# Turning 42 of 128 attention-probability blocks by DMA in a perceiver block, with GpSimd splitting and merging the 16-bit halves

## The reference, cut to what matters

```python
q, k, v = split_heads(LN(x) @ Wq + bq), split_heads(ctx @ Wk + bk), split_heads(ctx @ Wv + bv)
attn = softmax(einsum('bhqd,bhkd->bhqk', q, k) / sqrt(32))     # 2 x 16 x 128 x 2048
x = x + merge_heads(einsum('bhqk,bhkd->bhqd', attn, v)) @ Wo + bo
x = x + LN(self_attention(LN(x)) + LN(x)) * gamma + beta       # 16 heads, T = 128
x = x + LN(ffn_one_of_4_experts(x) + x) * gamma + beta         # 512 -> 2048 -> 512
```

## Time and profile before

| | |
|---|---|
| median of 3 runs (lowest to highest) | 510.3 us (509.75 to 511.0) |
| the profiled execution | 509.62 us, of which span 507.8 us |
| busy: PE, PE weight loads, DVE, ACT, POOL | 492.1, 380.6, 303.8, 265.0, 42.2 us |
| mean granted TensorE clock | 0.997 of full speed |

### The profile page before, as it was taken

One profiled execution on the slowest core, in us unless ns is written; L12 is line 12 of the kernel. 1 busy time (PEld: TensorE's weight loads), 2 busy tenths in 40 slices (PEclk: granted clock), 3 DMA queues, 4 the chain that ended last, 5 costly groups with the idle time before them and its releaser, 6 DMA issues.

```text
span 507.8 us, 9274 instructions
## 1 busy us (share of the span) xinstructions
PE 492.1 (97%) x3754; PEld 380.6 (75%) x3754; DVE 303.8 (60%) x585; ACT 265.0 (52%) x402; POOL 42.2 (8%) x34
## 2 busy tenths in 40 slices
PE   8999998999999999999999999989999999999995
PEld 6786777777777777898887777756686767888673
DVE  4637542645565452256168475668379988998932
ACT  4131027485767732327447757567337565677510
POOL 0220000000099000000000000000002010000000
PEclk9999999999999999999999999999999999999998
DMA  8900000000242002220120000099367799795000
GB/s 286 357 0 1 1 1 0 2 1 1 88 166 82 1 23 108 101 103 0 52 95 2 2 1 1 1 388 421 121 258 286 305 382 409 256 374 201 1 14 28
DMA packets 11353, 62.47 MB, mean 123 GB/s; under 512 B 1584, under 2 KB 2096, under 8 KB 4528
## 3 DMA queue, kind: packets, MB, share of 16 engines
q1 hardware_dynamic: 11024, 61.62, 31.7%
q10 hardware_dynamic: 288, 0.27, 0.2%
HBM read 61.36 MB, written 0.52 MB: 122 GB/s over the span
## 4 chain that ended last, share of the span: by engine, by line
PE 86%; ACT 7%; issue 3%; DVE 2%; POOL 0%; POOLq 0%; ACTq 0%; DVEq 0%
PE ps L1153 36%; PE ps L1223 11%; PE ps L1237 6%; PE ps L1207 6%; ACT Pm L453 4%; PE ps L1474 3%; PE ps L1476 3%; PE ps L1475 3%; PE ps L1418 3%; PE ps L1428 2%; PE ps L1430 2%; PE ps L1429 2%; PE ps L1147 1%; PE ps L1493 1%; ACT PT L461 1%
## 5 line engine op out<-in xcount | busy, mean ns | idle before, releaser
L752 DVE TENSOR_SCALAR_CACHE_REDUCE Pm<-ps,small 128x512 f32<-128x512 f32 x96 | 66.4, 749 | 30.4 <-PE ps L1207 30.3
L461 ACT COPY PT<-ps 128x512 f32<-128x512 f32 x128 | 68.5, 592 | 29.0 <-PE ps L1223 29.0
L1223 PE MATMUL ps<-ident,Pm 128*128 128x128 f32 x512 | 69.3, 277 | 3.2 <-ACT Pm L453 3.2
L1223 PEld LDWEIGHTS ps<-ident,Pm 128*128 128x128 f32 x512 | 56.5, 141 | 18.0 <-issue 11.0
L453 ACT ACTIVATE Pm<-Pm,small 128x2048 f32<-128x2048 f32 x32 | 64.3, 2010 | 3.5 <-DVE Pm L752 3.5
L732 DVE SCALAR_TENSOR_TENSOR KrL<-ps,small,KrH 128x512 fp32r<-128x512 f32 x32 | 23.9, 748 | 61.3 <-ACT KrH L439 61.3
L1153 PE MATMUL ps<-wvH,ctxH 128*128 128x512 f32 x124 | 50.6, 408 | 1.0 <-DVE V L741 1.0
L1153 PE MATMUL ps<-ctxH,wkH 128*128 128x512 f32 x124 | 51.1, 412 | 0.0
L1153 PE MATMUL ps<-ctxL,wkH 128*128 128x512 f32 x124 | 48.6, 392 | 0.0
L1153 PE MATMUL ps<-ctxH,wkL 128*128 128x512 f32 x124 | 48.5, 391 | 0.0
L1153 PE MATMUL ps<-wvH,ctxL 128*128 128x512 f32 x124 | 48.4, 390 | 0.0
(11 more groups left out here) (231 smaller groups left out, 876.6 us busy)
## 6 DMA issues: line engine op xcount, KB each, us to landing
w1raw<-in_W SPq DMA_DIRECT2D x16, 1024.0 KB, 6.1
w2raw<-in_W SPq DMA_DIRECT2D x15, 1024.0 KB, 5.0
raw<-in_ctxT SPq DMA_DIRECT2D x7, 1024.0 KB, 7.1
woF<-in_ffn_Wo SPq DMA_DIRECT2D x4, 1024.0 KB, 9.0
wo<-in_wo SPq DMA_DIRECT2D x2, 1024.0 KB, 4.7
ctx_first<-in_ctxT SPq DMA_DIRECT2D x4, 256.0 KB, 4.8
wv_raw<-in_xWv SPq DMA_DIRECT2D x2, 512.0 KB, 7.2
wq<-in_xWq SPq DMA_DIRECT2D x1, 1024.0 KB, 12.2
```

Source lines behind the costliest of these rows:

```text
L461: act.copy(PT[:, c % 2, i, :, :].rearrange("p k t -> p (k t)"), ps[:, t_bank(p, c, i), :]).then_inc(pt_done, 1)
L752: dve.tensor_scalar(Pm[:, i, c * CH:(c + 1) * CH], ps[:, i, :], -1.0, mx[:, p % 2, i, c - 1:c] if c else NOT_YET, ALU.mult, ALU.min, accum ...
L1223: last = pe.transpose(ps[:, t_bank(p, c, i), j * P:(j + 1) * P], Pm[:, i, c * CH + j * P:c * CH + (j + 1) * P], ident[:])
```

## The change

1. **Turns by DMA.** For passes 0 to 6, chunks 2 and 3 (`PEC` = 2), heads 0 to 2 (`HD` = 3), the turn is no longer made by TensorE. GpSimd takes the 512 floats of a head and chunk apart into 512 low and 512 high 16-bit halves (`probs_split`, into `stage`, one buffer for each of the two chunks), SyncE issues a DMA with transposition of the 128x1024 halves back into the same place of `Pm` (`turned`), and GpSimd puts the halves together again in `PT` (`probs_merged`). The next scores of that chunk now wait for the merge. Head 3 and chunks 0 and 1, and pass 7, stay as they were.
2. **Keys.** In rounds 1, 2, 3, 5, 6 and 7 VectorE makes the high part of chunks 0 and 1 too. The ring `KrH`, `KrL` has two slots in place of three.
3. **Second context.** ScalarE issues its loads and makes its high parts, VectorE the low parts, in halves, in gaps of rounds 3 and 4.
4. **Orders.** TensorE's weighted values of chunks 2 and 3 come at the start of the next round; 8 of the 12 matmuls of keys 0 of rounds 2, 3, 6 and 7 come before the last scores of the round before. VectorE makes keys 2 and 3 after the drains of chunks 0 and 1. Copies of `outputs2_T(0, ...)` move from VectorE to ScalarE. A few semaphores are merged.

```diff
-        KR = 3
+        KR = 2
+        stage = at("stage", [P, 2, 2, CH], U16, 184)
+        def by_dma(p, c, i):
+            return p < NP - 1 and c >= PEC and i < HD
+        def turned_before(p, c, i):
+            if p == NP - 1 or c < PEC:
+                return PE_TURNS * p + HPG * c + i
+            return PE_TURNS * p + HPG * PEC + (HPG - HD) * (c - PEC) + i - HD
+        def slot_user(p, c):
+            return C * p + c - 1
+        def halves_of(ap):
+            return ap.bitcast(U16).rearrange("p (n h) -> p n h", h=2)
 # SyncE
-            for c in range(C):
-                sp.wait_ge(k_mm, C * (G - 1) + c + 1)
-                sp.dma_start(raw[c][:], a["ctxT"][C + c]).then_inc(raw_in[c], 16)
+            def turned(p, i):
+                for c in range(PEC, C):
+                    sp.wait_ge(p_split, 2 * (HD * p + i) + c - PEC + 1)
+                    sp.dma_start_transpose(Pm[:, i, c * CH:(c + 1) * CH].bitcast(U16).rearrange("p (k t) -> p k t", t=T),
+                                           stage[:, c - PEC, :, :].rearrange("p h n -> p (h n)")).then_inc(p_turned[c], 16)
+            for p in range(G):
+                for i in range(HD):
+                    turned(p, i)
 ...
+            turned(G, 0)
             for k, w in enumerate(("wk", "wv")):
                 sp.wait_ge(qkv_mm[0], k + 1)
                 sp.dma_start(wS[:], a[w]).then_inc(wS_in, 16)
+                turned(G, k + 1)
 ...
+            for p in range(G + 1, NP - 1):
+                for i in range(HD):
+                    turned(p, i)
             sp.wait_ge(k_mm, NP * C)
             first_in_(0)
 # GpSimd
-            for c in range(C):
-                pool.wait_ge(raw_in[c], 32 if c else 16)
-                pool.tensor_copy(ctxH[c][:], raw[c][:]).then_inc(ctx_hi1, 1)
-                pool.wait_ge(ctx_hi1, c + 1)
-                pool.tensor_tensor(ctxL[c][:], raw[c][:], ctxH[c][:].bitcast(F32), ALU.subtract).then_inc(ctx_split1, 1)
+            def probs_split(p, i):
+                pool.wait_ge(exp_done, HPG * p + i + 1)
+                for c in range(PEC, C):
+                    if HD * p + i:
+                        pool.wait_ge(p_turned[c], 16 * (HD * p + i))
+                    words = halves_of(Pm[:, i, c * CH:(c + 1) * CH])
+                    pool.tensor_copy(stage[:, c - PEC, :, :], words.rearrange("p n h -> p h n")).then_inc(p_split, 1)
+            def probs_merged(p, c, i):
+                pool.wait_ge(p_turned[c], 16 * (HD * p + i + 1))
+                if i == 0:
+                    pool.wait_ge(pv_mm, slot_user(p, c))
+                words = halves_of(PT[:, c % 2, i, :, :].rearrange("p k t -> p (k t)"))
+                halves = Pm[:, i, c * CH:(c + 1) * CH].bitcast(U16).rearrange("p (h n) -> p h n", h=2)
+                pool.tensor_copy(words.rearrange("p n h -> p h n"), halves).then_inc(merged[c], 1)
+            for p in range(NP - 1):
+                probs_split(p, 0)
+                probs_split(p, 1)
+                if p == G + 1:
+                    rsqrt(LN3[0])
+                probs_split(p, 2)
+                for i in range(HD):
+                    probs_merged(p, PEC, i)
+                if p == G + 1:
+                    rsqrt(LN4[0])
+                for i in range(HD):
+                    probs_merged(p, PEC + 1, i)
+                if p == G - 1:
+                    rsqrt(LN2[0])
 # ScalarE: keys 0 and 1 only in round G; outputs2_T(0) takes all four heads
+            def context_in(c):
+                act.wait_ge(k_mm, C * (G - 1) + c + 1)
+                act.dma_start(raw[c][:], a["ctxT"][C + c]).then_inc(raw_in[c], 16)
+            def context_high(c, parts=(0, 1)):
+                act.wait_ge(raw_in[c], 32 if c else 16)
+                for h in parts:
+                    k = slice(HALF * h, HALF * (h + 1))
+                    act.copy(ctxH[c][:, k, :], raw[c][:, k, :]).then_inc(ctx_hi1, 1)
                 exponentials(p - 1, 0)
+                if p == G:
+                    context_high(3)
+                if p == G:
                     keys(p, 0)
+                if p == G - 1:
+                    context_in(0)
 ...
+                if p == G - 1:
+                    context_in(2)
+                    context_high(0, (0,))
 ...
+                            if p == G - 1:
+                                context_in(3)
 ...
+                    if p == G - 1 and c == 1:
+                        context_high(0, (1,))
+                    if p == G - 1 and c < 3:
+                        context_high(c)
 # VectorE
+                if p and p != G and c < 2:
+                    dve.wait_ge(k_mm, n + 1)
+                    dve.wait_ge(s_mm, (n - KR + 1) * HPG)
+                    dve.tensor_scalar(KrH[:, c % KR, :], ps[:, bank, :], bias3[:, 1, p % G:p % G + 1], None,
+                                      ALU.add).then_inc(k_hi, 1)
 ...
+                    if p and by_dma(p - 1, c, i):
+                        dve.wait_ge(merged[c], HD * (p - 1) + i + 1)
+                    elif p:
+                        dve.wait_ge(t_mm, turned_before(p - 1, c, i) + 1)
 ...
+            def context_low(c, parts=(0, 1)):
+                for h in parts:
+                    k = slice(HALF * h, HALF * (h + 1))
+                    dve.wait_ge(ctx_hi1, 2 * c + h + 1)
+                    dve.tensor_tensor(ctxL[c][:, k, :], raw[c][:, k, :], ctxH[c][:, k, :].bitcast(F32),
+                                      ALU.subtract).then_inc(ctx_split1, 1)
 ...
+                        if c < 2:
+                            keys(p, c + 2)
 # TensorE, a round with keys
+            EARLY = 8
 ...
+                    keys(p, 0, (EARLY if early_keys(p) else 0, 3 * KT))
                 if late:
+                    weighted_values(p - 2, C - 2)
                     weighted_values(p - 2, C - 1)
                     reciprocals_T(p - 2)
 ...
+                    probs_T(p - 1, 0, 0)
+                    probs_T(p - 1, 0, 1)
+                    keys(p, 2)
+                    probs_T(p - 1, 0, 2)
+                    probs_T(p - 1, 0, 3)
+                    scores(p, 0)
+                    probs_T(p - 1, 1, 0)
+                    probs_T(p - 1, 1, 1)
+                    weighted_values(p - 1, 0)
+                    probs_T(p - 1, 1, 2)
+                    probs_T(p - 1, 1, 3)
+                    scores(p, 1)
+                    weighted_values(p - 1, 1)
+                    keys(p, 3)
+                    probs_T(p - 1, 2, 3)
+                    if p == G + 3:
                         masks(0)
+                    scores(p, 2)
+                    probs_T(p - 1, 3, 3)
+                    if early_keys(p + 1):
+                        keys(p + 1, 0, (0, EARLY))
+                    scores(p, 3)
                 if p == G:
+                    while_values(0)
+                    weighted_values(p - 1, C - 2)
                     weighted_values(p - 1, C - 1)
-                    while_values(0)
```

More of the change, by code:

```diff
@@ L239, in perceiver_block @@
         s_mm, s_done = sem("s_mm"), sem("s_done")
+        p_split = sem("p_split")
+        merged = {c: sem(f"merged{c}") for c in range(PEC, C)}
+        p_turned = {c: sem(f"p_turned{c}") for c in range(PEC, C)}
         exp_done, t_mm = sem("exp_done"), sem("t_mm")
@@ L530, in values2, with outputs2_T @@
                 act.copy(V2[b][:].rearrange("p g d -> p (g d)"), ps[:, 4 * b, :]).then_inc(v2_ready, 1)
-            def outputs2_T(b):
+            def outputs2_T(b, heads):
                 act.wait_ge(cN_ready, b + 1)
-                for i in range(2, HPG):
+                for i in heads:
                     for a in range(HPG):
@@ L992, in alongside @@
                     outputs2(0)
[L993 to L996 removed]
+                if p == G + 1 and at_point == 3:
                     residual2(0)
@@ L1037, in _ @@
                     outputs(p - 2)
+                if p == G:
+                    context_low(3)
                 alongside(p, "keys1")
-                if p < NP:
-                    keys(p, 2)
                 for c in range(C):
@@ L1043, in _ @@
                         negative_scores(p, c)
-                        if c == 1:
-                            keys(p, 3)
+                        if p == G - 1 and c == 1:
+                            context_low(0, (1,))
+                        if c < 2:
+                            keys(p, c + 2)
+                        if p == G - 1 and c == 0:
+                            context_low(0, (0,))
+                        if p == G - 1 and c == 3:
+                            context_low(1)
                     if c == 2:
@@ L1154, in product, with keys @@
                 return mm
-            def keys(p, c):
+            def keys(p, c, part=(0, 3 * KT)):
                 b, g = divmod(p, G)
                 if b:
-                    pe.wait_ge(ctx_split1, c + 1)
+                    pe.wait_ge(ctx_split1, 2 * (c + 1))
                 else:
@@ L1169, in keys @@
```

(53 more changed lines are left out.)

93 lines of the change are left out of this document (46 added, 47 removed).

## The result

The changed kernel takes 503.52 us (four runs, 501.86 to 504.21), the one before, run beside it on the same chip, 510.48 (509.75 to 511.0). The ratio is 0.9864, with a 95% interval of 0.9848 to 0.9881: faster by 1.4%, 7.0 us. The forecast was 494.5, so the sign is right and the size is less than half of it. The profiled execution took 503.49 us with a span of 501.7; before these were 509.62 and 507.8. The sum of the prediction was -15.8 us against that execution, the measured difference is -6.1, and 9.7 us are to be explained.

A forecast was written before the change was run, and what follows sets the result against it. TensorE's own work was taken to bound each round. Against 509.6 us, -21.4 - 2.2 + 1.2 + 2.6 + 3.0 + 1.0 = -15.8 gave 493.8, or 494.5 for the median; range 488 to 514.

The forecast's parts named there:

- The turns' price: TensorE, seven passes: 42 turns leave at 0.51 us each, -21.4 us in all, 3.1 us a round.
- The stall before head 3: Rounds 1 to 3: TensorE's wait for exponentials before the turn of head 3 goes, -2.2 us.
- y: GpSimd's time for one split or merge copy of 1024 halves, taken as 1.0 us, upper bound 2.3.
- L: Landing time of one transposing DMA, taken as 4 us; beyond 5.2 each us costs 3 us a round in six rounds.
- rivals 2 and 3: Rounds: 2, round trip late, L 5.2 to 6.4, 506 us, chance 0.20; 3, slower, landing time, 520 us, chance 0.20.
- a sign of being wrong: Chunks 2 and 3: drains wait for GpSimd's merges, seen as TensorE idle before scores 3.
- The 56 ns of a piece: Transposing DMA: time per 256-byte piece from ScalarE's queue, giving 3.6 us for 1024 pieces, 5.6 with landing.
- 0.2 us a round: End of each round: last head of scores 3 waits for VectorE's drains until 23.9; +1.2 us in the sum.
- Weighted values and early keys are only moved.: TensorE's order: moving these pieces leaves its work unchanged, so no time was added or taken for it.
- the loads (1.5 for contention) and ScalarE's work (1.5): Round 3: context loads share DMA engines, +1.5; ScalarE's load issues +0.8 and high parts +0.7; +3.0 together, 0 to 6.
- The term of +2.6: Round 4: exponential 3 ends at 13.4, not 10.3, behind ScalarE's context part and keys; TensorE waits 3.0 instead of 0.4.
- the load term (0 to 2): Round 7: experts' loads start 5 to 6 us before the first product, not 10.1, and land in 6.1; +1.0 us.

The follow-up runs named there:

- filler run: Changed kernel plus eight needless one-block transposes on TensorE before the last scores of rounds 4 and 7: 501.23 us, ratio 0.9821 to the kernel before.

## Why the prediction was right and wrong

**Right: what bounds a steady round.** "A round is then 24.5 us of TensorE's work": round 2 is 24.57, TensorE busy for 24.52, and the forecast for it was 24.7. The turns' price holds in every round, -21.5 against -21.4. The stall before head 3 went.

**Right: the round trip is hidden in a steady round.** y was taken as 1.0 and is 1.04 at least, 1.16 on average for a split and 1.39 for a merge. L was taken as 4 and is 3.2. Both are far from the point where the cover is gone (L = 5.2), so rivals 2 and 3 did not come to be in the steady rounds. Round 3 is the exception: with landings of up to 6.3 us its drains of chunk 2 stood still for merges (they start 1.2 us apart in place of 0.67, and TensorE waits three times 0.7 us before the last scores), a sign of being wrong that the prediction named. The 56 ns of a piece were too high: the changed page's queues (packets, bytes in MB, share of sixteen engines) are
```profile
q1 hardware_dynamic: 54800, 68.44, 42.7%
q10 hardware_dynamic: 864, 4.46, 2.5%
```
and before they had 31.7% and 0.2%. So 45.2% of 501.7 less 31.9% of 507.8 is 64.8 us of sixteen engines for 42 x 1024 = 43,008 pieces, about 24 ns each (an estimate, for the shares are of whole kernels). The page's rule, beside which the prediction set 10.5 us for a DMA (the Trainium skill, "VectorE: DVE Perf Modes", The three transpose paths), is not borne out by this trace if blocks are taken one after another: eight land in 3.2 us, so they overlap.

**Wrong, 1: no term for the clock (6.6 us).** This is the largest step that failed. The forecast counted TensorE's work at 2.4 GHz throughout, since every window before had 1.00. It also accepted that TensorE would wait before the last scores ("the last head of scores 3 waits for that. That is tight"), and priced such a wait at 0.2 us a round. The waits themselves were 0.7 us in rounds 4 and 7 and 2.2 in round 3; what the half speed adds is 1.6 and 1.7 us there and 3.3 at round 3 (1.5 to 3.3 in the other runs that leave this round alone). The filler run shows cause and price for the first two; for round 3 the cause is argued from the likeness. Not every such wait does it. At the end of round 2 the last scores have one too (1.04 for four matmuls that take 0.50 elsewhere), and the 5 us behind it have a clock of 1.00 (the second fence is the window):
```profile
124.09 1.04 PE L1317 MATMUL ps<-KrH,qH 32*128 32x512 f32 x4
```
```profile
126.00:131.00 5.00, 5.00 (x79) 3.98 (x78) 3.60 (x10) 4.79 (x6) 2.02 (x2) 1.00 0.60 211
```
Before the clock fell TensorE had been busy for 3.34 of 5.00 us in round 3 (145.00 to 150.00), for 4.03 of 4.90 in round 4 and for 5.92 of 8.00 in round 7. Which waits suffice is open.

**Wrong, 2: "Weighted values and early keys are only moved."** The early keys are the cover of the chain at a round's end. Moved into rounds 1, 2, 5 and 6 they hide it; rounds 3 and 7 give theirs away and get none, round 4 keeps its keys whole. In the prediction's sum these rounds got the same 0.2 as the others. Round 7 has +2.9 left over, of which 1.5 were the masks (shown by their move). What remains of it, and 1.9 of round 4's +3.9 beside its slow keys, I put down to the missing cover. For round 4 a run shows it: with the product of the values in that place these 1.9 us are gone. For round 7 it is argued from the chain, for no run gave it early keys.

**Wrong, 3: round 3, +4.6 for +2.8.** The forecast named the loads (1.5 for contention) and ScalarE's work (1.5). It had nothing for VectorE's context parts in this round, and nothing for the clock, which is 1.3 of the +4.6. Loads are worth 1.3 (shown by leaving them out, within the 0.7 to 1.8 that the spread of this round between runs allows). Two chains end close together here: GpSimd's merges, four in 5.72 us after a landing of 6.3, and VectorE's drains with 3.0 us of context parts between them, which hold the round when the first is out of the way. Giving the whole of it back to the old order makes rounds 3 and 4 shorter by 3.5 us together with 3.1 us more of TensorE's work. How that divides between merges, context parts and clock was not taken apart.

**Right for another reason: round 4.** "so it ends at 13.4 and not 10.3, and TensorE waits 3.0": exponential 3 ends 13.3 us into the round, as worked out. But TensorE comes to it at the same moment, for it did keys 0 whole and at half speed (4.93), and waits for nothing. The term of +2.6 and the measured +3.9 are not the same thing. Where pass 2 was turned by TensorE, keys 0 of round 4 ran at full speed, and there the chain does go through ScalarE's exponentials, the last of which ends 13.0 us into the round; that round was 27.83.

**Wrong, 4: round 6, +1.7 for +0.2.** 1.03 of it is the statistics between `KrL` and the drains. They stood at the same point of VectorE's order before, and there the chain through the end of that round is TensorE alone: the drains had slack, which the new orders used up. My first guess at it, GpSimd's root, fell. The sum had the 0.2 of every round for it.

**Rest.** +1.3 beside +1.0 for the experts' loads: it was nearly all clock, for the filler took 1.5 away, and so the load term (0 to 2) was near nothing.

## What to carry to other kernels

When work is taken off the bounding engine, list for each border between stages what chain the other engines have there and which piece of the bounding engine's work covers it; a piece that is "only moved" may be that cover. A short wait of TensorE can cost more behind it than in it, so the granted clock of the stretch behind a wait is read before the wait is priced, and real work put in the gap can be worth more than its own length (3.7 us for a product of 2.75). Where a change needs a second rearrangement to make room (here the context's loads and parts), try it without that round: leaving pass 2 alone was better than turning it too.

## What the runs showed of the hardware

A DMA with transposition of 128x1024 halves of 16 bits within SBUF lands in 3.2 us (median of 42), in up to 4.9 outside round 3, and in round 3, beside loads of 1 MB, in up to 6.3 (7.6 in one run). GpSimd's strided copy of 1024 halves per partition takes 1.04 us into `stage` at best, 1.16 on average, and 1.39 on average into `PT`.

While GpSimd ran such copies, two small VectorE operations on two SBUF inputs took 1.23 and 1.16 us, which took 0.16 and 0.29 on average in the kernel before, and a context part of 128x1024 took 1.67 us where its neighbour had 1.22. The Trainium skill, "SBUF — State Buffer", SBUF: two separate sides, says that these two engines share one port pair that one of them holds alone for a whole instruction; the trace agrees, with the 0.9 and 1.1 us more of a small operation being about one GpSimd copy (1.04 to 1.39). For the two small operations it cost nothing here, as moving them showed: they then took 0.17 and 0.29, and round 7 was as long. The context parts stand between the drains of round 3, where it was not priced.
